# A new order inside the attention slots of an eight-core transformer layer

## Chip, cores and metric

The kernel runs on all eight cores of one Trainium2 chip. The time is that of the slowest core, in microseconds (us) on the device. The cores share nothing but the chip: each computes two of the sixteen sequences.

## The reference

The input is x of 16 sequences x 2048 tokens x 1024 features. One layer is computed:

```
n = layernorm(x)
Q, K, V = n@wq, n@wk, n@wv                        # 16 heads of 64
local   = softmax over a window of 256 earlier keys (blocks of 256) @ V
GQ, GK, GV = n@wgq, pool(n@wgk), pool(n@wgv)      # 8 heads of 64, 64 latents
rem     = softmax(GQ GK^T, causal over latents) @ GV @ r_out_w
out     = sigmoid(Q.gate_local) * local + sigmoid(Q.gate_remote) * rem
x       = x + out @ w_out
h = layernorm(x); for 3 blocks:                   # dequantized weights + lora
    h = linear(gelu(layernorm(linear(h)))) + h
x       = x + h
```

The weights of the feed-forward part are 4-bit integers with a scale for each group of 16, plus a product of two rank-32 matrices (lora).

## The kernel before

Each core works on 4096 tokens in eight tiles of 512 (`NJ = 8`, four to a sequence). There are three stages: the latent attention with its layernorm; the local attention (the stage of this change, about 355 to 1100 us of the span); and the feed-forward part. Every engine has a fixed list of instructions, written out by hand in the order of the source, and semaphores tie the lists together. An engine never passes over an instruction that waits.

The local attention goes through eight blocks, j = 0 to 7, one for each tile. A block begins with the values: eight units of eight matmuls (`values`, L451), with one unit for the gates (L483) in the middle. Then come eight slots, p = 0 to 7, one for each pair of heads; slot g = 8j + p. In a slot TensorE does, as far as the block has it:

- `bcast(g - 8)` (L427): two matmuls that spread the factors of the block before into S1, for VectorE's `mix`;
- `scores_a`, `scores_b`, `scores_c` of g + 1 (L361): key by query products with 64 rows of the array each, into S0, S1 and again S0;
- `project("k")` and `project("q")` (L349) of the next block, eight full-array matmuls each (blocks 0 to 6);
- `attend(g)` (L390 values, L399 denominators): matmuls with 64 columns of the array each, which need the masked exponentials of slot g;
- `lora` (L415), in slots 1 and 5, into S1: a weight slice for the feed-forward part;
- `wout(j - 2, p)` (L441): an eighth of the output projection of the block two before (blocks 2 to 7).

PSUM is shared out in units: S0 and S1 (1024 columns), O and D (512), and two units J0 and J1 of 512. k, q, wout, the values and the gates take J0 and J1 in turn, in the order of TensorE's list. Who takes a unit waits until its last user was read out (`drained`). k, q, values and the attention output are read out by ScalarE (`k_evac` L645, `evac` L592, L691, L711), the scores by its exponentials (`exp_a`, `exp_b`, `exp_p`, L656). wout is read out by VectorE (`resid`, L906: the addition of x, then statistics L908), which also masks the exponentials (`mask_a`, L863), multiplies by the broadcast factors (`mix`, L893, L894, L896), normalizes (`norm_a`, L918) and makes weight slices (`dequant_t` L925, `dequant_w` L934 or L944). ScalarE centres every other slice (`centre`, L674). After the eighth slot VectorE computes the factors of the block (`factor_a`, L876 to L885, with a reciprocal), and only then `resid(j - 2, 7)`.

SyncE's list (loads of x transposed and of the latent part, stores of x2 and its normalized form) and GpSimd's (loads of x and of weight slices) are the same in both kernels. They wait for `mixed`, `x2_done`, `xn2_done`, `dq_w` and `w_done`.

Of the kernel before, what the change touches and what calls it, by code (L numbers as in the profile page):

```python
# [20 lines left out]
NJ = NTOK // TT  # L21
# [13 lines left out]
A_K, A_Q, A_V, A_P = 0, 6144, 10240, 16384  # L35
# [38 lines left out]
def build_program():  # L74
# [38 lines left out]
    with contextlib.ExitStack() as es:  # L113
# [30 lines left out]
        a = lambda o, n: AR[:, o:o + n]  # L144
# [24 lines left out]
        junit = {}  # L169
# [84 lines left out]
        def pe(t):  # L254
# [89 lines left out]
            def project(kind, w, j, p):  # L344
                u = junit[kind, j, p] = nextj()
                k = u.take(kind, j, p)
                t.wait_ge(u.drained, k)
                for c in range(8):
                    mm = t.matmul(u.ap, w(c, p * 128, 128), xt(j % 2, c), start=(c == 0), stop=(c == 7))  # L349
                mm.then_inc(u.filled)  # L350
# [54 lines left out]
            def lora(n):  # L405
                i, c = DQ[n]
                lp = 32 * (i % 4)
                if n == 0:
                    t.wait_ge(ld_ca, 16 * 13)
                if n == 32:  # L410
                    t.wait_ge(ld_lalb2, 32)
                k = S1.take("lo", n)
                t.wait_ge(S1.drained, k)
                for hf in range(2):
                    mm = t.matmul(S1.ap[:, hf * 512:hf * 512 + 512], LALB[lp:lp + 32, c * 128:c * 128 + 128],  # L415
                                  LALB[lp:lp + 32, 1024 + hf * 512:1024 + hf * 512 + 512], start=True, stop=True)
                mm.then_inc(S1.filled)

            def bcast(g):

                j, p = divmod(g, 8)
                if p == 0:
                    t.wait_ge(f_done, j + 1)
                k = S1.take("bc", g)
                t.wait_ge(S1.drained, k)
                for side in range(2):
                    mm = t.matmul(S1.ap[:, side * 512:side * 512 + 512],  # L427
                                  SEL[:, (2 * p + side) * 128:(2 * p + side) * 128 + 128], a(A_F, 512),
                                  start=True, stop=True)
                mm.then_inc(S1.filled)  # L430
# [44 lines left out]
            for j in range(NJ):  # L475
                for n in range(8):
                    values(j, n)
                    if n == 3:
                        u = junit["z", j] = nextj()
                        k = u.take("z", j)  # L480
                        t.wait_ge(u.drained, k)
                        for c in range(8):
                            mm = t.matmul(u.ap, GZ[:, c * 128:c * 128 + 128], a(A_Q + c * 512, 512),  # L483
                                          start=(c == 0), stop=(c == 7))
                        mm.then_inc(u.filled)
                if j + 1 < NJ:
                    t.wait_ge(ld_xt[(j + 1) % 2], 16 * ((j + 1) // 2 + 1))
                for p in range(8):
                    g = 8 * j + p
                    if j >= 1:  # L490
                        bcast(g - 8)
                    if g + 1 < 8 * NJ:
                        scores_a(g + 1)
                    if j + 1 < NJ:
                        project("k", wk, j + 1, p)
                    if g + 1 < 8 * NJ:
                        scores_b(g + 1)
                    if p == 0:
                        for n in (6, 7):
                            u = junit["v", j, n]  # L500
                            t.wait_ge(u.drained, u.nth["v", j, n])
                    attend(g)
                    if g + 1 < 8 * NJ:
                        scores_c(g + 1)
                    if p in (1, 5):
                        lora(2 * j + p // 4)
                    if j + 1 < NJ:
                        project("q", wq, j + 1, p)
                    if j >= 2:
                        wout(j - 2, p)  # L510


            def y1(s, oc):
# [75 lines left out]
        def act(s):  # L589
# [95 lines left out]
            for j in range(NJ):  # L685
                for n in range(8):
                    u = junit["v", j, n]
                    tc, hf = divmod(n, 2)
                    vo = A_V + vslot(j, tc) * 1024 + hf * 512
                    s.wait_ge(u.filled, u.nth["v", j, n])  # L690
                    s.activation(a(vo, 512), u.ap, AF.Identity).then_inc(u.drained)  # L691
                    if n == 3:
                        u = junit["z", j]
                        s.wait_ge(u.filled, u.nth["z", j])
                        if j >= 1:
                            s.wait_ge(f_done, j)
                        s.activation(f32v(A_EZ, 512), u.ap, AF.Exp, scale=-1.0).then_inc(u.drained)
                for p in range(8):
                    g = 8 * j + p
                    if g + 1 < 8 * NJ:  # L700
                        exp_a(g + 1)
                    if j + 1 < NJ:
                        k_evac(j + 1, p)
                    if g + 1 < 8 * NJ:
                        exp_b(g + 1)
                    if p % 2 == 0 and 4 * (j - 2) + p // 2 - 1 >= 0:
                        rstd_a(4 * (j - 2) + p // 2 - 1)
                    if j >= 1:
                        s.wait_ge(mixed, g - 7)
                    s.wait_ge(UO.filled, UO.nth["av", g])  # L710
                    s.activation(a(A_O + p * 512, 512), UO.ap, AF.Identity).then_inc(UO.drained)  # L711
                    if g + 1 < 8 * NJ:
                        exp_p(g + 1, S0, "sc", 1024, 0)
                    if p == 2:
                        centre(2 * j)
                    if j + 1 < NJ:
                        evac(junit["q", j + 1, p], ("q", j + 1, p), a(A_Q + p * 512, 512))


            def y1_evac(sn, oc):  # L720
# [53 lines left out]
        def dve(v):  # L774
# [198 lines left out]
            for j in range(NJ):  # L973
                for p in range(8):
                    g = 8 * j + p
                    if j >= 1:
                        mix(g - 8)
                    if j >= 2 and p >= 1:
                        resid(j - 2, p - 1)
                    if p in (1, 5):  # L980
                        dequant_t(2 * j + p // 4)
                    if g + 1 < 8 * NJ:
                        mask_a(g + 1)
                    if p % 2 == 0 and 4 * (j - 2) + p // 2 - 1 >= 0:
                        norm_a(4 * (j - 2) + p // 2 - 1)
                    if p in (1, 5):
                        dequant_w(2 * j + p // 4)
                factor_a(j)
                if j >= 2:
                    resid(j - 2, 7)  # L990


            def square(sn, c):
# [384 lines left out]
```

## Time and profile before

| | |
|---|---|
| median of 3 runs | 1890.48 us (1888.58 to 1891.98) |
| the profiled execution | 1895.78 us, span of its slowest core 1894.3 us |
| spans of the eight cores | 1878.3 to 1894.3 us |
| VectorE busy | 1014.5 us, 54% |
| ScalarE busy | 837.0 us, 44% |
| load of 128 rows of x, issue to landing | 6.6 us |
| store of 128 rows of x2, issue to landing | 2.8 us |
| load of the scales of a weight slice, issue to landing | 8.4 us |

All rows are of core 0, the slowest. Matmuls are pipelined: 512 columns are issued every 0.22 us though one lasts 0.38. So starts are compared, not ends. Some matmul records are missing (a run of eight can show as x7).

A window's row gives: from and to, length, busy time of PE, PEld, DVE, ACT and POOL with their instructions, granted clock (1.00 is 2.4 GHz, and time at 1.2 GHz pulls it down), share of the DMA engines, GB/s. A timeline's row gives start, length, engine, line, shapes and count, and in brackets the idle time before it and who ended it.

### The profile page before, as it was taken

What the parts mean: (1) busy time and instruction counts of PE and PEld (TensorE: products, weight loads), DVE (VectorE), ACT (ScalarE), POOL (GpSimd) and SP (SyncE); (2) the same over time, 40 slices, a digit from 0 to 9 for tenths busy, and PEclk for the clock granted to TensorE, in tenths of its full rate; (3) what the DMA queues carried; (4) which work ended last, traced back from release to release, by engine and by line L of the source; (5) the groups of instructions that cost most, each with busy time, mean ns of one, the idle gap of its engine ahead of it and who ended that gap; (6) DMA issues with size and microseconds to landing.
All of it is one profiled execution on the core that took longest, in us unless ns stands there. A gap on an engine that the chain in (4) does not pass through costs nothing.

```text
span 1894.3 us, 26192 instructions; the slowest of 8 cores (1878.3 to 1894.3 us)
## 1 busy us (share of the span) xinstructions
PE 1606.5 (85%) x8828; PEld 722.4 (38%) x8994; DVE 1014.5 (54%) x1473; ACT 837.0 (44%) x1224; POOL 108.0 (6%) x191
## 2 busy tenths in 40 slices
PE   0347689999998989889875878999999899999998
PEld 0123233444443434444332333334434344444444
DVE  1346575044464656474656754555545656565555
ACT  0123345466454535445452145454444544444442
POOL 2000200000000000000000000000010000000000
PEclk9878899999999999999998989999999999999999
DMA  9986754611223233231358381211121121032223
GB/s 150 157 130 135 144 142 156 130 41 51 54 69 79 69 78 100 58 89 43 81 93 185 88 155 36 48 41 44 28 62 29 28 56 42 15 111 90 100 101 123
DMA packets 134353, 162.55 MB, mean 86 GB/s; under 512 B 80608, under 2 KB 92304, under 8 KB 131024
## 3 DMA queue, kind: packets, MB, share of 16 engines
q1 hardware_dynamic: 100128, 97.02, 19.1%
q0 software_dynamic: 34096, 63.85, 18.9%
q8 instruction: 76, 1.25, 0.3%
q14 instruction: 53, 0.43, 0.1%
HBM read 123.91 MB, written 52.43 MB: 93 GB/s over the span
## 4 chain that ended last, share of the span: by engine, by line
PE 58%; DVE 15%; DVEq 6%; issue 6%; DMA 6%; SPq 5%; ACT 5%; ACTq 0%; POOL 0%; POOLq 0%
PE ps L524 14%; PE ps L349 10%; PE ps L451 6%; PE ps L549 6%; PE ps L554 4%; SPq L1192 4%; DMA XT<-AR 4%; PE ps L441 3%; DVE AR L1004 3%; PE ps L361 3%; DVEq L931 2%; PE ps L532 2%; PE ps L390 2%; PE ps L399 2%; DVE WA L809 2%
## 5 line engine op out<-in xcount | busy, mean ns | idle before, releaser
L524 PE MATMUL ps<-WA,WB 128*128 128x512 bf16 x1003 | 234.2, 389 | 27.2 <-ACT AR L724 21.8
L349 PE MATMUL ps<-XT,WA 128*128 128x512 bf16 x967 | 231.2, 381 | 7.8 <-issue 7.1
L656 ACT ACTIVATE AR<-ps 128x1024 bf16<-128x1024 f32 (+2 forms) x192 | 186.1, 970 | 99.9 <-PE ps L361 97.7
L740 ACT ACTIVATE AR<-AR,LNB,LNG 128x512 bf16<-128x512 bf16 x192 | 145.6, 806 | 154.0 <-DVE AR L1004 153.8
L724 ACT ACTIVATE AR<-ps,CB 128x512 bf16<-128x512 f32 x192 | 128.8, 683 | 181.3 <-PE ps L524 181.3
L290 PE MATMUL ps<-XT,WB 128*128 128x512 bf16 x254 | 69.0, 438 | 129.2 <-DMA XT<-AR 129.0
L524 PEld LDWEIGHTS ps<-WA,WB 128*128 128x128 bf16 x1024 | 101.0, 100 | 155.7 <-issue 45.4
L592 ACT ACTIVATE AR<-ps 128x512 bf16<-128x512 f32 x96 | 57.3, 597 | 207.3 <-PE ps L290 158.1
L863 DVE TENSOR_TENSOR AR<-AR,MLOC 128x3072 bf16<-128x3072 bf16 x48 | 84.4, 1759 | 109.9 <-ACT AR L656 109.9
L451 PE MATMUL ps<-WA,XT 128*128 128x512 bf16 x509 | 122.8, 400 | 23.6 <-DVE AR L906 23.5
L349 PEld LDWEIGHTS ps<-XT,WA 128*128 128x128 bf16 x1024 | 91.2, 98 | 121.5 <-issue 27.9
L441 PE MATMUL ps<-WA,AR 128*128 128x512 bf16 x503 | 123.2, 390 | 16.5 <-DVE AR L906 15.6
L1012 DVE SCALAR_TENSOR_TENSOR WA<-ps,BIAS,WA 128x512 bf16<-128x512 f32 x128 | 95.7, 748 | 76.3 <-PE ps L549 76.2
L554 PE MATMUL ps<-XT,AR 128*128 128x512 bf16 x498 | 121.6, 385 | 8.2 <-DVE AR L1028 4.0
L999 DVE TENSOR_TENSOR AR<-AR 128x512 bf16<-128x512 bf16 x192 | 73.5, 422 | 100.3 <-ACT AR L724 99.4
L925 DVE SCALAR_TENSOR_TENSOR AR<-AR 128x1024 f32<-128x1024 int8 x48 | 58.3, 1219 | 127.8 <-DMA AR<-scT 127.8
L1004 DVE TENSOR_TENSOR AR<-AR 128x512 bf16<-128x512 bf16 x192 | 123.5, 686 | 6.1 <-issue 6.1
L524 PE MATMUL ps<-WA,AR 128*128 128x512 bf16 x503 | 114.3, 383 | 13.1 <-ACT AR L724 12.6
L549 PE MATMUL ps<-AR,XT 128*128 128x512 bf16 x500 | 116.4, 379 | 4.1 <-DVE WA L1012 3.5
L549 PE MATMUL ps<-AR 128*128 128x512 bf16 x499 | 116.2, 379 | 4.1 <-DVE WA L1012 3.5
L893 DVE TENSOR_TENSOR AR<-ps,AR 128x512 bf16<-128x512 f32 x64 | 44.2, 690 | 115.9 <-PE ps L427 115.1
L290 PEld LDWEIGHTS ps<-XT,WB 128*128 128x128 bf16 x256 | 27.7, 110 | 170.1 <-issue 148.8
(134 smaller groups left out, 1988.6 us busy)
## 6 DMA issues: line engine op xcount, KB each, us to landing
AR<-scT POOLq DMA_DIRECT2D x48, 512.0 KB, 8.4
AR<-x_in POOLq DMA_DIRECT2D x64, 256.0 KB, 6.6
y<-AR SPq DMA_DIRECT2D x32, 512.0 KB, 2.9
xnT<-XT SPq DMA_DIRECT2D x8, 1024.0 KB, 3.9
remT<-AR SPq DMA_DIRECT2D x8, 1024.0 KB, 6.2
XT<-xnT SPq DMA_DIRECT2D x8, 1024.0 KB, 5.3
AR<-remT SPq DMA_DIRECT2D x64, 128.0 KB, 3.5
x<-AR SPq DMA_DIRECT2D x32, 256.0 KB, 2.8
```

What stands on the lines that cost most here:

```text
L290: mm = t.matmul(u.ap, WB[:, c * 512 + oc * 128:c * 512 + oc * 128 + 128], xt(par, c), start=(c == 0), stop=(c == 7))
L349: mm = t.matmul(u.ap, w(c, p * 128, 128), xt(j % 2, c), start=(c == 0), stop=(c == 7))
L441: mm = t.matmul(u.ap, a(A_MIX + (j % 2) * 4096 + c * 512 + sub * 128, 128), wo(c, hf * 512, 512), start=(c == 0), stop=(c == 7))
L451: mm = t.matmul(u.ap, xt(j % 2, c, tc * 128, 128), wv(c, hf * 512, 512), start=(c == 0), stop=(c == 7))
L524: mm = t.matmul(u.ap, wmat(2 * k3, c, oc * 128, 128), rt(tt, c), start=(c == 0), stop=(c == 7))
L549: mm = t.matmul(u.ap, wmat(2 * k3 + 1, c, oc * 128, 128), a(yb + c * 512, 512), start=(c == 0), stop=(c == 7))
L554: t.matmul(u.ap, a(yb + c * 512 + sub * 128, 128), wmat(5, c, hf * 512, 512), start=(c == 0), stop=False)
L656: s.activation(dst[:, :, col + lo:col + hi], src[:, :, lo:hi], AF.Exp, scale=ISQ).then_inc(u.drained)
L724: s.activation(a(B_Y1 + (sn % 2) * 4096 + oc * 512, 512), u.ap, AF.Identity, bias=CB[:, 8 * i + oc:8 * i + oc + 1]).then_inc(u.drained)
L740: s.activation(yb, yb, AF.Gelu, bias=LNB[:, 8 * i + c:8 * i + c + 1], scale=LNG[:, 8 * i + c:8 * i + c + 1]).then_inc(g_done)
L1004: v.tensor_tensor(yb, yb, f32v(B_RS, 512), op=ALU.mult).then_inc(yn_done)
L1012: v.scalar_tensor_tensor(rt(tt, oc), u.ap, BIAS[:, 8 * i1 + oc:8 * i1 + oc + 1], rt(tt, oc), op0=ALU.add, op1=ALU.add).then_inc(u.drained)
```

## The change

The order inside a slot is rewritten on three engines. TensorE does the output unit, k, lora and q right after the broadcast, then scores a and b, the attention, scores c. ScalarE does the statistics of the second layernorm, k, q and the centring first, then the exponentials a and b, the attention output, c. VectorE adds the residual of the slot's own output unit, not of the slot before, so that the eighth one comes in slot 7, ahead of `factor_a`; `dequant_w`, `norm_a` and, in slot 7, `factor_a` go before the mask, and `dequant_t` moves from slots 1 and 5 to the ends of slots 0 and 4.

```diff
@@ TensorE
                     if j >= 1:
                         bcast(g - 8)
+                    if j >= 2:
+                        wout(j - 2, p)
+                    if j + 1 < NJ:
+                        project("k", wk, j + 1, p)
+                    if p in (1, 5):
+                        lora(2 * j + p // 4)
+                    if j + 1 < NJ:
+                        project("q", wq, j + 1, p)
                     if g + 1 < 8 * NJ:
                         scores_a(g + 1)
-                    if j + 1 < NJ:
-                        project("k", wk, j + 1, p)
-                    if g + 1 < 8 * NJ:
                         scores_b(g + 1)
...
                     attend(g)
                     if g + 1 < 8 * NJ:
                         scores_c(g + 1)
-                    if p in (1, 5):
-                        lora(2 * j + p // 4)
-                    if j + 1 < NJ:
-                        project("q", wq, j + 1, p)
-                    if j >= 2:
-                        wout(j - 2, p)
@@ ScalarE
                     g = 8 * j + p
+                    if p % 2 == 0 and 4 * (j - 2) + p // 2 - 1 >= 0:
+                        rstd_a(4 * (j - 2) + p // 2 - 1)
+                    if j + 1 < NJ:
+                        k_evac(j + 1, p)
+                        evac(junit["q", j + 1, p], ("q", j + 1, p), a(A_Q + p * 512, 512))
+                    if p == 2:
+                        centre(2 * j)
                     if g + 1 < 8 * NJ:
                         exp_a(g + 1)
-                    if j + 1 < NJ:
-                        k_evac(j + 1, p)
-                    if g + 1 < 8 * NJ:
                         exp_b(g + 1)
-                    if p % 2 == 0 and 4 * (j - 2) + p // 2 - 1 >= 0:
-                        rstd_a(4 * (j - 2) + p // 2 - 1)
                     if j >= 1:
                         s.wait_ge(mixed, g - 7)
                     s.wait_ge(UO.filled, UO.nth["av", g])
                     s.activation(a(A_O + p * 512, 512), UO.ap, AF.Identity).then_inc(UO.drained)
                     if g + 1 < 8 * NJ:
                         exp_p(g + 1, S0, "sc", 1024, 0)
-                    if p == 2:
-                        centre(2 * j)
-                    if j + 1 < NJ:
-                        evac(junit["q", j + 1, p], ("q", j + 1, p), a(A_Q + p * 512, 512))
@@ VectorE
                     if j >= 1:
                         mix(g - 8)
-                    if j >= 2 and p >= 1:
-                        resid(j - 2, p - 1)
+                    if j >= 2:
+                        resid(j - 2, p)
                     if p in (1, 5):
-                        dequant_t(2 * j + p // 4)
+                        dequant_w(2 * j + p // 4)
+                    if p % 2 == 0 and 4 * (j - 2) + p // 2 - 1 >= 0:
+                        norm_a(4 * (j - 2) + p // 2 - 1)
+                    if p == 7:
+                        factor_a(j)
                     if g + 1 < 8 * NJ:
                         mask_a(g + 1)
-                    if p % 2 == 0 and 4 * (j - 2) + p // 2 - 1 >= 0:
-                        norm_a(4 * (j - 2) + p // 2 - 1)
-                    if p in (1, 5):
-                        dequant_w(2 * j + p // 4)
-                factor_a(j)
-                if j >= 2:
-                    resid(j - 2, 7)
+                    if p in (0, 4):
+                        dequant_t(2 * j + p // 4)
```

## Rows read from the trace of the kernel before

**Rows 1.** The page, busy time of TensorE, its share of the span.
```profile
PE 1606.5 (85%) x8828; PEld 722.4 (38%) x8994; DVE 1014.5 (54%) x1473; ACT 837.0 (44%) x1224; POOL 108.0 (6%) x191
```

**Rows 2.** Windows, core 0: values after block 0; slots 1, 2; values; slots 4; values; slots 7.
```profile
421.12:436.66 15.54, 15.49 (x73) 7.02 (x73) 7.46 (x6) 5.37 (x9) 0.00 (x0) 1.00 0.01 1
436.66:495.88 59.22, 53.71 (x429) 25.03 (x436) 30.89 (x38) 38.09 (x49) 2.36 (x4) 0.97 0.24 63
...
511.43:579.42 67.99, 65.94 (x493) 30.97 (x500) 44.12 (x59) 39.94 (x56) 3.95 (x7) 1.00 0.33 86
579.42:602.12 22.70, 17.93 (x73) 7.54 (x73) 7.04 (x8) 4.78 (x8) 0.00 (x0) 0.85 0.05 12
...
691.63:755.35 63.72, 62.19 (x434) 28.49 (x441) 42.04 (x67) 35.59 (x58) 4.48 (x8) 1.00 0.40 102
...
936.11:957.97 21.86, 17.09 (x73) 7.26 (x73) 7.04 (x8) 4.78 (x8) 0.00 (x0) 0.92 0.05 14
957.97:1015.70 57.73, 39.15 (x347) 19.95 (x352) 40.23 (x55) 28.39 (x38) 3.14 (x6) 0.94 0.81 139
```
**Rows 3.** Timeline of TensorE, first slot of block 5: start, length, line, count.
```profile
777.72 0.39 PE L361 MATMUL ps<-AR 64*128 64x384 bf16 x4
778.05 1.90 PE L349 MATMUL ps<-XT,WA 128*128 128x512 bf16 x7
779.88 0.39 PE L361 MATMUL ps<-AR 64*128 64x256 bf16 x4
780.20 0.85 PE L390 MATMUL ps<-AR 128*64 128x256 bf16 x12
780.88 0.82 PE L399 MATMUL ps<-AR,OHD 128*64 128x256 bf16 x12
781.64 0.39 PE L361 MATMUL ps<-AR 64*128 64x384 bf16 x4
781.96 1.90 PE L349 MATMUL ps<-XT,WA 128*128 128x512 bf16 x8
783.70 1.89 PE L441 MATMUL ps<-WA,AR 128*128 128x512 bf16 x8
```

**Rows 4.** Timeline of ScalarE, the same slot, and the centring of slot 2.
```profile
780.04 0.60 ACT L645 ACTIVATE AR<-ps 128x512 bf16<-128x512 f32 x1 [0.81 <-PE ps L349]
780.54 1.02 ACT L656 ACTIVATE AR<-ps 128x1024 bf16<-128x1024 f32 x1
781.44 0.29 ACT L667 ACTIVATE RST<-MV,COLS 128x1 f32<-128x1 f32 x1
...
781.95 0.60 ACT L711 ACTIVATE AR<-ps 128x512 bf16<-128x512 f32 x1
782.44 1.02 ACT L656 ACTIVATE AR<-ps 128x1024 bf16<-128x1024 f32 x1
...
801.24 1.15 ACT L674 ACTIVATE WB<-AR,RSUM 128x1024 bf16<-128x1024 f32 x1
```

**Rows 5.** Timeline of VectorE, mask of the first slot to the scale product of the second.
```profile
783.56 1.76 DVE L863 TENSOR_TENSOR AR<-AR,MLOC 128x3072 bf16<-128x3072 bf16 x1 [3.85 <-ACT AR L656]
785.24 0.54 DVE L918 TENSOR_SCALAR AR<-AR,MV,RST 128x1024 bf16<-128x1024 bf16 x1
786.13 0.69 DVE L893 TENSOR_TENSOR AR<-ps,AR 128x512 bf16<-128x512 f32 x1 [0.35 <-PE ps L427]
786.73 0.68 DVE L894 TENSOR_TENSOR AR<-ps,AR 128x512 bf16<-128x512 f32 x1
...
787.86 0.68 DVE L906 TENSOR_TENSOR AR<-ps,AR 128x512 bf16<-128x512 f32 x1
...
789.24 1.21 DVE L925 SCALAR_TENSOR_TENSOR AR<-AR 128x1024 f32<-128x1024 int8 x1
```

**Rows 6.** Timeline of VectorE, end of block 5, behind the factor chain: the eighth residual.
```profile
850.97 0.68 DVE L906 TENSOR_TENSOR AR<-ps,AR 128x512 bf16<-128x512 f32 x1
```

**Rows 7.** Timeline of TensorE, the second unit of values after block 5.
```profile
851.80 7.85 PE L451 MATMUL ps<-WA,XT 128*128 128x512 bf16 x24 [4.72 <-DVE AR L906]
```

## The prediction

> **What bounds the kernel now.** I read the page first: PE is busy for 85% of the span [rows 1], so I took PE's order of work for the clock of the attention stage and asked where it stands still. The windows of the stage, cut at the starts of the value matmuls, answer that [rows 2]. A stage of eight slots of blocks 2 to 6 takes 68.0 us (63.7 in block 4, where a sequence starts and less is masked), PE is busy for 97% of them, at clock 1.00. The values stage after blocks 0 and 1 takes 15.5 us; the five that follow blocks 2 to 6 take 22.70 (first) to 21.86 us (last), 111.0 together, although the same 72 matmuls run: in each, PE stops after its first unit for 4.4 to 4.85 us [rows 7] and runs on at a lower clock (0.85 to 0.92 over the stage). The row names VectorE's L906, the residual addition of the eighth output unit. VectorE started it only behind the factor chain [rows 6]. So two things can be won: these gaps, and small seams inside a slot. I then wrote down one slot by the timelines of the three engines [rows 3 to 5], because what decides is whether the new order leaves ScalarE and VectorE time to answer.
>
> **The change on PE.** Eight full-array matmuls in a row take 1.74 us (781.96 to 783.70), but 1.83 when half-array scores follow, and scores worth 0.22 us of columns take 0.33 before a full-array run [rows 3]. A seam between full-array and half-array work costs 0.10 us. Before, a slot has six: broadcast to scores a, a to k, k to b, b to values, denominators to c, c to q. After, four: q to a, b to values, denominators to c, c to the next broadcast. 0.2 us a slot, over the 56 slots of blocks 0 to 6 11 us, less one seam more for each of 14 lora pairs (1.4): about 10 us. Row and rule: the Trainium skill, "TensorEngine Tiling (Array Packing)", section Key Properties, says that a change of tiling mode drains TensorE. The trace agrees, with 0.10 us; by that rule alone the change only wins, and this is the first rival below.
>
> New slot of PE, from the first q matmul: q 1.74, seam 0.10, scores a and b 0.22 each, seam 0.10, values 0.68, denominators with seam 0.76, last scores with seam 0.32 [rows 3]: 4.14, then two broadcasts 0.43, output unit 1.74, k 1.74. Without a wait that is 8.05 us.
>
> **What the other two need.** ScalarE's order is now k, q, scores a, scores b, attention output, scores c. Counted from the start of q: its evacuation starts 2.00 later (k: 778.05 to 780.04), the exponential of a 0.50 after that, b 0.90 after a, the output evacuation 0.90 after b, c 0.49 after that: 4.79 [rows 3, 4]. It lasts 1.02, and the mask starts 1.12 after its start (782.44 to 783.56): 5.91. The next VectorE instruction starts 1.68 later: 7.59 [rows 5]. That is the mix of the next slot, for the mask is queued ahead of it on VectorE. From the mix's first product to the residual's addition are 1.73 us (786.13 to 787.86): 9.32. PE goes on 0.83 after the start of such an addition (850.97 to 851.80) [rows 6, 7]: 10.15.
>
> What waits for that addition? The two J units alternate. Output unit, k and q are taken in turn, so q of a slot has the unit that this slot's output matmuls filled, and waits for their residual. Before, the residual of an output unit had until the q matmuls of the next slot; now it has only the 1.74 us of k, and lies behind mask and mix. So from q to q a slot of blocks 2 to 6 takes 10.15 us, 2.1 above PE's own 8.05. Behind the waiting q on PE stand the scores and the attention of the slot, so the exponentials start late too, and the next mask with them: the loop closes. Part of that shows ahead of the broadcast: its unit S1 is freed by the exponential of b, which ends 3.40 + 1.02 after q, plus 0.15 to PE (851.80 less the end of the 0.68 us addition), 4.57 against 4.14.
>
> Extras in a block: the scale product of a weight slice (1.21 us, [rows 5]) stands between mask and mix after slots 0 and 4: 2.4. Centring (L674, 1.15 us, the next start some 1.05 later, [rows 4]) stands ahead of the exponentials in slot 2: 1.05. The lora pair and its VectorE step lie within the wait. Block: 3.91 to the first q, 7 x 10.15 = 71.05, 3.5, and 4.14 after the last q: 82.6 against 68.0: +14.6, four times 58.4. Block 4 scaled by 63.7/68.0: +13.7. Together +72.1.
>
> **Queues of the DMAs.** The residual comes a slot earlier, so loads of x have less time: a tile's load can go once the norm of two tiles before is stored, some two slots (20 us) ahead, and store and load take 2.8 + 6.6 us in the page. A weight slice is loaded after the centring of slot 2 and wanted at the end of slot 4, again 20 us against 8.4. SyncE's and GpSimd's lists are the same; I cost this at nothing. Were slots to shrink under 5 us it would show.
>
> Block 1 has no output unit. There the wait on S1 paces it: 4.57 + 0.43 + 1.74 = 6.74 from q to q, five times. In slots 1 and 5 lora waits for the mix to free S1: 7.59 + 1.21 + 0.60 + 0.68 + 0.15 = 10.23, and 0.53 to q: 10.76, twice. With 2.17 ahead, 4.14 behind and centring 1.05: 62.6 against 59.22 [rows 2]: +3.4. Bounds: -3 if the waits for lora vanish, +6 if the clock falls behind them.
>
> Block 0: seams -1.6 and centring ahead of the exponentials +1.1: -0.5. Block 7 has no projections: PE already waits there for the mix to free S1, 57.73 us at clock 0.94 [rows 2]; the cycle scores b, exponential, output, c, mask, mix is the same in both orders (about 6.45 us), and the weight step moves from the broadcast's wait to that of scores b. I take 0, bounds -4 and +4. The tail after it is tied to stores and loads of x that keep their order: 0, bounds -3 and +3.
>
> **What is won.** The residual of the eighth unit now goes before the factor chain, so its J unit is free before the values start. The five values stages return to 15.54 us: 111.0 - 77.7 = -33.3. What is late next there: the masks of the next block now follow the chain, but the attention that needs them comes 17 us later; nothing.
>
> **Clock.** Blocks 2 to 6 will stand for a fifth of the time. The rows show 1.00 where PE is busy for 97%, 0.97 at 91% (block 1) and 0.94 at 68% (block 7) [rows 2]. I take 0.96 for them: 3.3 us of PE's work more in a block, of which some fifth (q, of the slot's work) lies on the cycle: +3 in all. Bounds 0 and +20.
>
> Sum: 72.1 + 3.4 - 0.5 - 33.3 + 3 = +45, to 1940.5 on the profiled execution (1895.8 us, 1.5 beyond its span). That is 5.3 above the median of the runs, so I forecast 1935 as median. Its own range, 1912 to 1965.
>
> **Rivals.** (1) Seams and gaps only: the addition is never awaited, PE runs through. Then 33 + 10 are won: 1847. For it: VectorE has slack, since it is busy for some 6 of 8 us. Against: slack isn't order; the mask ends at 7.6 after q whatever the load. Decides: whether mask ends before the next output unit does (6.7 after q). Chance 3%.
> (2) Only the wait on S1 is left, because the residual is there in time: ScalarE or VectorE runs its short list faster than the sum of starts above. Slots of 4.57 + 3.91 = 8.48: block 3.91 + 59.4 + lora 1.3 + 1.05 + 4.14 = 69.8, +1.8 in five blocks, 9 in all; with +3.4 - 0.5 - 33.3: 1869, faster than before. The point from which it decides: the cycle must be under 8.9 us, where a block takes 11.55 + 7 x 8.9 = 73.8, 5.8 more than before, five times 28, and the gaps pay for it. Chance 8%.
> (3) The clock falls with the waits. A stall of 2.1 us a slot comes just ahead of q, and if all 35 q runs on the cycle go at 1.2 GHz instead of 2.4, each costs 1.74 more: +61, 1993. Against it: block 7 waits 1.2 to 3.1 us in every slot and keeps 0.94. The Trainium skill, "TensorE: Matmul & The Clock Gate", section "A second HAM failure mode: psum-queue depth-cycling", describes this: short idle spells between matmul groups make the clock swing. Chance 7%.
> (4) PE's seams and orders cancel, no change: a cycle of about 8.9. Chance 3%.
>
> **Numbers.** Forecast 79%. 1908 to 1965 leaves out rivals 1 to 3 and little of the forecast. A difference under 0.2% (3.8 us) can't be told from none. Faster: rivals 1 and 2, 11%. Same: 3%. Slower: the rest, 86%.
>
> **What would show it.** Right: in slots of blocks 2 to 6 PE waits 1.6 to 1.8 us before L349 (q) for DVE L906, and about 0.4 before L427 for ACT L656; first q to first q of the next slot 10.1 us; slots' stages near 82.6 us; no wait before L451, values stages 15.5 us; VectorE's L893 starts right behind L863. Wrong: L906 starts as soon as the output unit is full, or the waits stand at the scores.

## The result, and the profile after

The changed kernel takes 1961.17 us (median of four runs, 1957.38 to 1969.89), the kernel before 1890.48 on the same chip (median of three): a ratio of 1.038 (95% interval 1.033 to 1.043), slower. The forecast was 1935, its range 1908 to 1965. All comparisons leave runs out in which the cores of one die were disturbed.

The profiled execution took 1957.38 us. Its slowest core is core 1, with a span of 1955.9 us; all rows of after are of that core. In its numbering L903 is the addition of the residual (L906 before), L890 and L891 the first two products of the mix, L860 the mask, L655 an exponential, L922 the scale product and L941 the weight step. First the page's busy line, which answers to [rows 1].

```profile
PE 1621.1 (83%) x8994; PEld 726.9 (37%) x8994; DVE 1010.3 (52%) x1473; ACT 828.4 (42%) x1224; POOL 108.0 (6%) x191
```

TensorE's share fell by only two points and VectorE has no more work than before. Nothing here says where 70 us went. The windows do; they are cut at the same places as [rows 2]: slots of blocks 0 and 1, slots 2, values, slots 4, 5 and 7.

```profile
372.93:421.67 48.74, 45.17 (x362) 21.24 (x360) 15.18 (x21) 31.89 (x56) 2.36 (x4) 1.00 0.18 55
...
437.22:504.93 67.71, 58.93 (x438) 27.18 (x436) 30.39 (x38) 35.98 (x49) 2.36 (x4) 0.90 0.18 55
...
520.48:603.95 83.47, 68.51 (x502) 32.03 (x500) 42.93 (x61) 36.62 (x54) 3.95 (x7) 0.98 0.27 73
603.95:619.50 15.55, 15.55 (x77) 7.07 (x74) 7.56 (x6) 6.48 (x11) 0.00 (x0) 1.00 0.00 1
...
718.40:797.84 79.44, 66.84 (x442) 29.20 (x440) 41.23 (x69) 32.26 (x56) 4.48 (x8) 0.96 0.32 87
...
813.39:898.96 85.57, 69.78 (x502) 32.37 (x500) 43.38 (x62) 36.89 (x56) 4.48 (x8) 0.96 0.30 81
...
1013.53:1078.77 65.24, 44.85 (x361) 21.63 (x359) 41.87 (x59) 28.11 (x38) 2.79 (x5) 0.82 0.81 127
```

Every values stage now takes 15.54 or 15.55 us. Every stage of slots is longer. The same cuts on core 1 of both kernels give this account; the slots' stages of before agree on all eight cores within 0.4 us, its long values stages within 1. The changed kernel's do not: over the cores slots 1 take 64.0 to 67.7 us, slots 5 83.8 to 85.8, slots 7 62.5 to 66.0.

| stage | before | after | difference | predicted |
|---|---|---|---|---|
| slots 0 | 45.8 | 48.7 | +2.9 | -0.5 |
| slots 1 | 59.3 | 67.7 | +8.4 | +3.4 |
| slots 2 to 6 | 335.5 | 415.3 | +79.8 | +72.1, clock +3 |
| slots 7 | 57.8 | 65.2 | +7.4 | 0 |
| values behind blocks 2 to 6 | 111.6 | 77.7 | -33.9 | -33.3 |
| sum | | | +64.6 | +45 |

The spans of core 1 differ by 72.5 us. Of the other 7.9, the feed-forward part holds 5.3 and the tail after slot 7 the rest. One part of the row of slots 7 is no loss: the stage ends with the last attention, and the eighth output unit (1.74 us) lay behind that point before and lies ahead of it now. Like with like, block 7 lost 5.7 us and the tail 1.7 more than the cut shows. On core 0 the feed-forward part goes the other way (835.3 us before, 827.2 after), so I count it as spread between executions and not as the change's.

An ordinary slot of block 2 (no lora pair) answers to [rows 3]. TensorE's timeline, from its broadcast to the k matmuls of the next slot:

```profile
561.54 0.59 PE L427 MATMUL ps<-AR,SEL 128*128 128x512 bf16 x2 [0.37 <-ACT AR L655]
561.97 1.89 PE L441 MATMUL ps<-WA,AR 128*128 128x512 bf16 x8
563.70 1.89 PE L349 MATMUL ps<-XT,WA 128*128 128x512 bf16 x8
567.13 1.89 PE L349 MATMUL ps<-XT,WA 128*128 128x512 bf16 x8 [1.54 <-DVE AR L903]
568.95 0.61 PE L361 MATMUL ps<-AR 64*128 64x384 bf16 x8
...
573.84 1.89 PE L349 MATMUL ps<-XT,WA 128*128 128x512 bf16 x8
```

ScalarE's in the same slot:

```profile
569.11 0.60 ACT L591 ACTIVATE AR<-ps 128x512 bf16<-128x512 f32 x1 [2.83 <-PE ps L349]
569.61 1.94 ACT L655 ACTIVATE AR<-ps 128x1024 bf16<-128x1024 f32 x2
...
571.89 1.06 ACT L655 ACTIVATE AR<-ps 128x1024 bf16<-128x1024 f32 x1
```

And VectorE's:

```profile
562.91 1.76 DVE L860 TENSOR_TENSOR AR<-AR,MLOC 128x3072 bf16<-128x3072 bf16 x1 [4.96 <-ACT AR L655]
564.58 0.68 DVE L890 TENSOR_TENSOR AR<-ps,AR 128x512 bf16<-128x512 f32 x1
...
566.30 0.68 DVE L903 TENSOR_TENSOR AR<-ps,AR 128x512 bf16<-128x512 f32 x1
...
573.05 1.76 DVE L860 TENSOR_TENSOR AR<-AR,MLOC 128x3072 bf16<-128x3072 bf16 x1 [4.83 <-ACT AR L655]
```

Follow the loop: q starts at 567.13, its evacuation at 569.11, the exponentials at 569.61, the last of them at 571.89, the mask at 573.05. In the slot before, the mask started at 562.91, the mix 1.67 later, the addition 1.72 after that, and q 0.83 after the addition. The loop is 5.92 + 1.67 + 1.72 + 0.83 = 10.14 us, and from k to k TensorE takes 10.14. VectorE stands idle for almost 5 us ahead of each mask: the engine on which everything waits is itself waiting half of the time.

The groups of waits on TensorE, 355 to 1080 us. In PSUM (ps), L349 is q, L415 lora, L427 the broadcast, L361 the scores; the numbers are total us, count, longest:

```profile
PE ps L349 <- DVE AR L903: 42.9, 35, 1.9
PE ps L415 <- DVE AR L891: 30.9, 14, 6.0
PE ps L427 <- ACT AR L655: 10.0, 26, 0.5
PE ps L361 <- ACT AR L655: 7.2, 8, 1.1
```

In the slots with a lora pair, 1 and 5, the wait is divided in two, and the q matmuls behind it often run at the lower clock. Slot 1 of block 5:

```profile
827.43 0.59 PE L415 MATMUL ps<-LALB 32*128 32x512 bf16 x2 [1.55 <-DVE AR L891]
828.55 3.40 PE L349 MATMUL ps<-XT,WA 128*128 128x512 bf16 x8 [0.53 <-DVE AR L903]
```

The eight q matmuls took 3.40 us, not 1.89. On core 1 q is slow (2.7 to 3.6 us) in 7 of the 10 lora slots of blocks 2 to 6, and never behind the 25 undivided waits of 1.3 to 1.9 us. Added up it costs 9.1 us, all of it in the loop (4.9 to 9.1 over the cores).

### The profile page after: what moved, and what is told of

Read it like the earlier page. It is cut to its first block, busy times and chain, and to the rows that moved or that the text cites. A ratio compares the mean times of both kernels' runs of the same rounds, so it can differ in the third digit from the quotient of the medians.

```text
span 1955.9 us, 26358 instructions; the slowest of 8 cores (1932.5 to 1955.9 us)
## 1 busy us (share of the span) xinstructions
PE 1621.1 (83%) x8994; PEld 726.9 (37%) x8994; DVE 1010.3 (52%) x1473; ACT 828.4 (42%) x1224; POOL 108.0 (6%) x191
## 4 chain that ended last, share of the span: by engine, by line
PE 49%; DVE 14%; DVEq 9%; ACT 8%; issue 7%; DMA 7%; SPq 5%; ACTq 1%; POOL 0%; POOLq 0%
PE ps L523 13%; PE ps L349 9%; PE ps L451 6%; PE ps L548 5%; DVEq L892 4%; PE ps L553 4%; SPq L1188 4%; ACT AR L655 4%; DMA XT<-AR 4%; DVE AR L1000 3%; PE ps L531 2%; PE ps L390 2%; DVEq L904 2%; PE ps L361 2%; PE ps L274 1%
## 5 line engine op out<-in xcount | busy, mean ns | idle before, releaser
L349 PE MATMUL ps<-XT,WA 128*128 128x512 bf16 x1024 | 249.5, 393 | 42.9 <-DVE AR L903 42.9
L655 ACT ACTIVATE AR<-ps 128x1024 bf16<-128x1024 f32 (+2 forms) x192 | 181.6, 979 | 34.0 <-PE ps L361 33.6
L860 DVE TENSOR_TENSOR AR<-AR,MLOC 128x3072 bf16<-128x3072 bf16 x48 | 84.3, 1757 | 187.1 <-ACT AR L655 187.1
L349 PEld LDWEIGHTS ps<-XT,WA 128*128 128x128 bf16 x1024 | 99.1, 100 | 180.2 <-issue 75.6
L922 DVE SCALAR_TENSOR_TENSOR AR<-AR 128x1024 f32<-128x1024 int8 x48 | 58.4, 1221 | 134.0 <-DMA AR<-scT 133.8
L451 PE MATMUL ps<-WA,XT 128*128 128x512 bf16 x512 | 113.2, 379 | 0.0
L361 PE MATMUL ps<-AR 64*128 64x384 bf16 (+1 forms) x704 | 67.8, 287 | 21.5 <-ACT AR L655 7.2
```

The lines of the kernel that those rows point to most:

```text
L361: mm = t.matmul(u.ap[:, hh * 512 + col:hh * 512 + col + nq * 128], AR[rows, kcl:kcl + 128], AR[rows, A_Q + p * 512 + q0 * 128:A_Q + p * 51 ...
L451: mm = t.matmul(u.ap, xt(j % 2, c, tc * 128, 128), wv(c, hf * 512, 512), start=(c == 0), stop=(c == 7))
L655: s.activation(dst[:, :, col + lo:col + hi], src[:, :, lo:hi], AF.Exp, scale=ISQ).then_inc(u.drained)
```

## Experiments

Each ratio is to the kernel before on the same chip, with its 95% interval. The first four ran on one chip, the next three on one, the last two on one.

### 1. The residual ahead of the factor chain alone

The kernel before, with the one move on VectorE that frees the eighth output unit.

```diff
-                factor_a(j)
                 if j >= 2:
                     resid(j - 2, 7)
+                factor_a(j)
```

> The kernel before with one edit: the residual of the eighth output unit goes ahead of the factor chain. By my account the five gaps of the values stages (4.4 to 4.85 us each, and the slow clock behind them) go: each values stage 15.5 us instead of 21.7 to 22.9, in sum 33 us, so about 1857 us, and the slots stay at 68.0 us a block. The rival, that the gap is made by the attention's end or by the evacuations and the residual only closes it, gives 1885 to 1891 us with another wait ahead of the second values unit.

Measured: 1861.8 and 1865.4 us, ratio 0.982 (0.975 to 0.989). Windows of core 3, slots 2 and the values behind them:

```profile
509.62:577.61 67.99, 67.20 (x501) 30.96 (x500) 43.70 (x58) 39.98 (x56) 3.95 (x7) 1.00 0.32 86
577.61:593.15 15.54, 15.54 (x73) 7.06 (x72) 7.63 (x8) 4.79 (x8) 0.00 (x0) 1.00 0.07 19
```

Beside [rows 2], the slots are the same to 0.01 us and the values lose their gap, at clock 1.00. This half of the change is worth some 33 us, as computed (about 1857 us was forecast). So the rest of it costs about 100.

### 2. The mask behind the mix and the residual

The loop's longest link taken out: VectorE adds the residual before it masks.

```diff
                     if j >= 2:
                         resid(j - 2, p)
+                    if g >= 1:
+                        mask_a(g)
...
-                    if g + 1 < 8 * NJ:
-                        mask_a(g + 1)
```

> The changed kernel with one edit on VectorE: the mask of a slot's exponentials goes behind that slot's mix and residual instead of ahead of them (the same instructions, one place later in the list). If the loop mask, mix, residual, q is what costs, q no longer waits for the residual; what is left is the broadcast's wait for the exponential of scores b, so q to q falls from 10.15 to about 8.5 us, a block's slots from 83.6 to about 70, block 1 from 67.6 to about 56, block 7 from 65 to about 50: 1865 to 1875 us. If instead the loss comes from the burst of scores on PE and ScalarE or from the clock, and the wait for the residual is only where it shows, the waits turn up elsewhere and the time stays within 10 us of 1961.

Measured: 1885 us (1879.0 to 1888.9), ratio 0.994 (0.991 to 0.996). Windows of core 3, slots 1, 2 and 7, and a group of waits:

```profile
437.79:494.22 56.43, 52.28 (x438) 25.70 (x436) 32.08 (x39) 35.63 (x48) 2.36 (x4) 1.00 0.24 66
...
509.77:580.99 71.22, 66.22 (x501) 32.24 (x500) 45.11 (x62) 37.41 (x55) 3.94 (x7) 1.00 0.33 86
...
937.93:1014.84 76.91, 48.41 (x361) 24.30 (x359) 45.66 (x62) 28.90 (x40) 4.47 (x8) 0.82 0.65 122
...
PE ps L390 <- DVE AR L860: 20.1, 8, 4.1
```

One move on one engine takes 12 to 15 us from each of blocks 2 to 6 (83.5 to 71.2 in block 2): the mask's place is the cause of the loop. The 76 us between this kernel and the changed one (84 by the two ratios, for they ran on different chips) are the largest effect of any single edit here. The forecast, 1865 to 1875 us, missed because of block 7, where I had expected 50 us and 77 came (73.7 to 77.0 over the cores). There is no projection there to cover the mask: the attention itself now waits for it (six of the eight waits, 19.5 us, are in block 7), scores b wait 4.5 us for the weight step in each of slots 1 and 5, and the clock fell to 0.82.

### 3. The output unit behind q

The other way to open the loop: TensorE fills the J unit only after q has taken its own.

```diff
-                    if j >= 2:
-                        wout(j - 2, p)
...
                     if j + 1 < NJ:
                         project("q", wq, j + 1, p)
+                    if j >= 2:
+                        wout(j - 2, p)
```

> The changed kernel with one edit on TensorE: the output unit is computed behind q instead of ahead of k, so it is the q of the next slot that takes its J unit, 8 us later. VectorE's order stays as it is, mask ahead of mix. By the theory that the J unit carries the loop, the wait of q for the residual is gone and the slots of blocks 2 to 6 are paced by the broadcast's wait for scores b, 8.3 to 8.5 us a slot: some 80 us less in five blocks, 1880 us; blocks 1 and 7 keep their waits for S1 (67.6 and about 65 us). By the rival that mask ahead of mix costs the slot anyway through S1 (scores b then wait for the mix), slots stay near 10 us and the time near 1955 us.

Measured: 1984.6 us, ratio 1.046 (1.041 to 1.052): the forecast of 1880 missed by over 100. TensorE on core 0, two output units in a row, then the lora pair and scores b of slot 1:

```profile
555.52 1.89 PE L441 MATMUL ps<-WA,AR 128*128 128x512 bf16 x8
...
563.80 1.89 PE L441 MATMUL ps<-WA,AR 128*128 128x512 bf16 x8
...
573.80 0.59 PE L415 MATMUL ps<-LALB 32*128 32x512 bf16 x2 [3.29 <-DVE AR L891]
...
583.22 0.40 PE L361 MATMUL ps<-AR 64*128 64x256 bf16 x4 [3.26 <-DVE AR L941]
```

And VectorE in that slot:

```profile
579.74 0.69 DVE L903 TENSOR_TENSOR AR<-ps,AR 128x512 bf16<-128x512 f32 x1 [5.57 <-PE ps L441]
...
581.85 1.22 DVE L941 SCALAR_TENSOR_TENSOR AR<-AR,ps 128x1024 bf16<-128x1024 f32 x1 [0.31 <-issue]
```

The ordinary slot did what I had worked out (8.28 us, no wait before q anywhere), which confirms the J unit as the link. But I had not followed slots 1 and 5. There the weight step that frees S1 is queued on VectorE behind the residual, the residual waits 5.57 us for the output unit, which is now late, and scores b wait for S1. The slot takes 17.1 us. On core 1, the slowest, the clock goes to between 0.87 and 0.90 in four of the five blocks (0.94 in block 4), a block takes up to 90.4 us, and block 7 takes 75.0 us in place of 65.2.

### 4. An order without the loop

TensorE in blocks 2 to 6: output unit, k, broadcast, q, scores a and b, attention, scores c, and lora last. VectorE: residual's addition, mask, mix, statistics, norm, scale product and weight step.

```diff
@@ TensorE
-                    if j >= 1:
+                    if j == 1 or j == NJ - 1:
                         bcast(g - 8)
...
                         project("k", wk, j + 1, p)
-                    if p in (1, 5):
-                        lora(2 * j + p // 4)
+                    if 2 <= j < NJ - 1:
+                        bcast(g - 8)
...
                         scores_c(g + 1)
+                    if p in (1, 5):
+                        lora(2 * j + p // 4)
@@ VectorE
-                    if j >= 1:
+                    if j == 1 or j == NJ - 1:
                         mix(g - 8)
                     if j >= 2:
-                        resid(j - 2, p)
...
+                        resid_x(j - 2, p)
+                    if g >= 1:
+                        mask_a(g)
+                    if 2 <= j < NJ - 1:
+                        mix(g - 8)
```

> A version that should beat both. In blocks 2 to 6 TensorE does output unit, k, broadcast, q, scores a and b, attention, scores c, lora; VectorE adds the residual first, then masks, then mixes, with the statistics last; blocks 1 and 7 keep the broadcast first with mask behind mix; centring goes to the end of ScalarE's slot, both steps of a weight slice to the end of VectorE's. By the sum of starts no wait is left in a slot of blocks 2 to 6 except about 0.5 us ahead of lora: 8.1 us a slot, 66 to 67 us a block, values stages 15.5, together 1840 to 1850 us. If PE's bursts or ScalarE set a floor that I don't see, slots stay at 8.5 us or more and the time at 1865 or above.

Measured: 1848.9, 1854.4 and 1862.1 us (1840 to 1850 was forecast), ratio 0.978 (0.971 to 0.984). On core 5, windows of slots 2 and 7, and a group of waits (L862 is the mask here):

```profile
511.51:577.55 66.04, 65.30 (x502) 32.12 (x500) 44.78 (x62) 36.50 (x54) 3.95 (x7) 1.00 0.32 87
...
916.08:985.77 69.69, 42.39 (x362) 22.98 (x361) 45.28 (x62) 28.64 (x40) 4.46 (x8) 0.88 0.89 136
...
PE ps L390 <- DVE AR L862: 24.2, 8, 8.3
```

Slots 2 take 66.0 us, 2.0 under [rows 2], and an ordinary slot 8.02 us, where the prediction had 8.05 for TensorE without waits. So the gain of fewer seams is real: some 2 us a block, 8.7 in five blocks (326.8 us on core 5 against 335.5). Block 7 gives that back, for its attention waits for the masks, as in experiment 2. Part of the loss has another cause: on the three cores (0, 3, 4) where no load of x came late, block 7 takes 61.3 to 63.4 us, on the others 65.8 to 70.9. On core 5 the residual, which is queued ahead of the mask, waits 6.0 us for a load of x, and the longest wait above, 8.3 us, is the one behind it.

### 5 and 6. Load on VectorE off and on the loop

One more pass over 128 x 1024 elements in every slot of blocks 2 to 6, written to room that nothing reads: ahead of the mask in 5 (shown), where VectorE is idle, and right behind it in 6.

```diff
+                    if 2 <= j < NJ - 1:
+                        v.drain()
+                        v.tensor_tensor(a(A_D2, 1024), MLOC[:, 0:1024], MLOC[:, 0:1024], op=ALU.mult)
                     if g + 1 < 8 * NJ:
                         mask_a(g + 1)
```

> The changed kernel with one more pass of VectorE (128x1024 bf16 product into unused room, about 0.7 us with the drain before it) in each slot of blocks 2 to 6, put ahead of the mask, that is, behind the residual and its statistics, where VectorE waits for the exponentials. If the cycle mask, mix, residual, q sets the pace, this pass isn't on it: the slots stay at 10.14 us and the time within 5 us of the changed kernel's (1957 to 1965 us). If VectorE's amount of work is what counts, it costs the same as the next kernel's pass, 25 us.

Measured: 1963 us, ratio 1.035 (1.033 to 1.037), against 1.038 for the change without the pass. Core 1, the waits before q:

```profile
PE ps L349 <- DVE AR L903: 42.3, 35, 1.9
```

Forty passes cost nothing: blocks 2 to 6 take 413.1 us on this core, 415.3 without the passes, and over the eight cores the means are 414.1 and 413.9. (Block 7 took 72.5 us on this core, for the scales of a weight slice came 8.5 us late; on the other cores it took 62.7 to 67.7.)

> The same pass, put behind the mask, that is, between mask and mix. By the theory each of the 35 steps from q to the next q in blocks 2 to 6 grows by the whole pass and its drain, 0.7 to 0.9 us: 25 to 32 us more, 1985 to 1995 us, the slots at 10.9 to 11.0 us. If there is slack on the cycle, less than 10 us more.

Measured: 2007 us, ratio 1.058 (1.056 to 1.060): 44 us more than experiment 5 on the same chip, where 25 to 32 was forecast. The groups of waits before q and before lora, core 1:

```profile
PE ps L349 <- DVE AR L903: 61.7, 35, 2.6
PE ps L415 <- DVE AR L891: 37.1, 14, 4.4
```

And the q matmuls of one slot, core 3:

```profile
576.91 2.74 PE L349 MATMUL ps<-XT,WA 128*128 128x512 bf16 x8 [2.34 <-DVE AR L903]
```

An ordinary slot takes 10.93 us in place of 10.14: the pass and the drain before it, 0.79 us, are paid in full. So the place on VectorE sets the time, not the load. On core 1 blocks 2 to 6 take 458.3 us, 43.0 more than in the changed kernel. Forty slots at 0.79 are 31.6 of that. The rest is the clock: behind waits of 2.34 us the q matmuls shown took 2.74 us in place of 1.89, and such slow groups add up to 21.0 us on core 1, 11.9 more than in the changed kernel. The five stages have a granted clock of 0.93 to 0.96 on core 3.

### 7. Blocks 0, 1 and 7 one by one

Experiment 4, with lora ahead of q in blocks 0 and 1, and in block 7 the order of the kernel before on TensorE and VectorE.

```diff
+                    if j < 2 and p in (1, 5):
+                        lora(2 * j + p // 4)
...
+                    if j == NJ - 1:
+                        wout(j - 2, p)
```

> The new order of e4 in blocks 2 to 6 (66.0 us of slots), block 1 with lora ahead of q as in e2 (56.4 us there, 59 to 61 in e4), block 7 in the order of the kernel before with its eighth residual ahead of the factors (57.8 us there, 61 to 71 in e4, where the attention waited for a mask behind the mix). By the sum 3 us less in block 1 and 4 to 10 in block 7: 1844 to 1850 us. If block 7's time is set by the loads of the transposed operand that share its stretch and not by the order, it stays above 61 us and the time at e4's 1858.

Measured: 1857.8 us, ratio 0.980 (0.978 to 0.982), where 1844 to 1850 was forecast. Block 7 takes 64.5 us, not 58. ScalarE's timeline, core 0, the statistics, which stand ahead of the exponentials:

```profile
952.19 0.29 ACT L672 ACTIVATE RST<-MV,COLS 128x1 f32<-128x1 f32 x1 [5.42 <-DVEq L920]
```

I had put two engines back and left the third. ScalarE still has the layernorm's statistics at the head of the slot, ahead of the exponentials, and they wait 5.42 us for a residual that VectorE, in the old order, adds a slot later.

### 8. Block 7 in the old order on all three engines

Experiment 4, with block 7 as before and the eighth residual ahead of the factor chain.

```diff
-                    if p % 2 == 0 and 4 * (j - 2) + p // 2 - 1 >= 0:
+                    if p % 2 == 0 and 4 * (j - 2) + p // 2 - 1 >= 0 and j < NJ - 1:
                         rstd_a(4 * (j - 2) + p // 2 - 1)
...
                         exp_b(g + 1)
+                    if p % 2 == 0 and j == NJ - 1:
+                        rstd_a(4 * (j - 2) + p // 2 - 1)
```

> e4 with block 7 in the order of the kernel before on all three engines (output unit last, mask of the next slot behind the mix, ScalarE's statistics behind the exponentials), its eighth residual ahead of the factors. e7 had this on TensorE and VectorE only, and its first exponential of a slot stood behind statistics that now come later: 64.5 us. If the order is what sets block 7, it returns to 57 to 61 us, against 61 to 70 in e4, and the time of the slowest core falls from 1858 to 1846 to 1852 us. If the clock or the loads of the transposed operand set it, the block stays above 62 us and the time within 3 us of e4's.

Measured: ratio 0.977 (0.971 to 0.982), 1851.4 to 1878.2 us. Window of slots 7, core 4:

```profile
920.13:980.06 59.93, 42.92 (x354) 20.52 (x353) 40.20 (x56) 28.39 (x38) 2.79 (x5) 0.89 0.80 135
```

The stage is back at 59.2 to 60.4 us over the cores, as forecast. This order has the eighth output unit behind the cut again, so it compares with 57.8 us before and with 63.5 (65.2 less 1.74) in the changed kernel: most of block 7's loss is that of the order. The time is not as forecast: 1846 to 1852 us was forecast, and the median of the six runs is 1858.8. The kernel as a whole can't be told from experiment 4. The two are the fastest here, but their intervals overlap that of experiment 1, too.

### 9. The scale product off the lora path

The changed kernel, with the scale product of a weight slice next to its weight step, so that it no longer stands ahead of the mix.

```diff
                     if p in (1, 5):
+                        dequant_t(2 * j + p // 4)
                         dequant_w(2 * j + p // 4)
...
-                    if p in (0, 4):
-                        dequant_t(2 * j + p // 4)
```

> The changed kernel with the scale product of a weight slice (1.21 us) taken from behind the mask of slots 0 and 4 and put ahead of the weight step in slots 1 and 5. By the theory the waits of lora for the mix fall by 1.2 us each (3.3 to 2.1 us in blocks 1 and 7), but scores b then wait some 1.2 us longer for the weight step in the same slots, so that blocks 2 to 6 gain at most 1.5 us each; the 2.67 us for which VectorE waited for a weight slice in block 7 go too. Sum: 5 to 15 us less than 1961, 1946 to 1956. If lora's waits come from somewhere else than VectorE's order, they stay at 3.3 us and the time at 1961.

Measured: 1952.4 us (1946.3 to 1958.3), ratio 1.026 (1.021 to 1.032). TensorE in block 1 of the changed kernel, a lora pair and the q matmuls behind it:

```profile
449.54 1.01 PE L415 MATMUL ps<-LALB 32*128 32x512 bf16 x2 [3.28 <-DVE AR L891]
450.48 3.59 PE L349 MATMUL ps<-XT,WA 128*128 128x512 bf16 x8
```

The same in this experiment, with the window of slots 1:

```profile
449.92 0.59 PE L415 MATMUL ps<-LALB 32*128 32x512 bf16 x2 [2.15 <-DVE AR L891]
450.44 1.90 PE L349 MATMUL ps<-XT,WA 128*128 128x512 bf16 x8
...
438.74:499.03 60.29, 53.30 (x437) 25.72 (x436) 30.40 (x38) 35.65 (x49) 2.36 (x4) 1.00 0.22 61
```

On this core two waits are 1.13 us shorter each, 2.3 together, but block 1 is 7.4 us shorter. The other 5 are the clock: behind both waits of 3.28 us eight matmuls took 3.59 us, at the lower of its two levels, and behind both of 2.15 they took 1.90. The stage's clock went from 0.90 to 1.00. But the shorter wait did not settle it. On six of the eight cores of the same execution one of the two groups still ran slowly, as on core 0:

```profile
447.54 0.59 PE L415 MATMUL ps<-LALB 32*128 32x512 bf16 x2 [2.15 <-DVE AR L891]
448.06 3.55 PE L349 MATMUL ps<-XT,WA 128*128 128x512 bf16 x8
```

Block 1 takes 60.3 to 61.9 us over the cores, and 64.0 to 67.7 in the changed kernel. In its blocks 2 to 6 the waits ahead of lora fell to 0.4 us, and no q group behind a lora pair was slow.

## Why the prediction was right, and by how much it missed

The forecast was 1935 us and 1961 came: 26 us short, of which 20 lie in the attention stage as core 1 shows it.

**The mechanism** was right, step for step. Evacuation 2.00 us after q was predicted and 1.98 measured; mask 5.91 and 5.92; mix 1.68 later and 1.67; residual 1.73 and 1.72; q 0.83 and 0.83; the loop 10.15 and 10.14. The broadcast waits 0.37 us for the exponential of b, about 0.4 predicted; q waits 1.54, just under the 1.6 to 1.8 predicted. Experiments 2 (mask moved: the wait goes), 3 (output unit moved: the ordinary slot is 8.28 us) and 6 (a pass on the loop: paid in full) each break or stretch one link, and 5 excludes VectorE's load.

**The gaps** ahead of the values: -33.3 predicted, -33.9 measured, and alone in experiment 1. **The seams**: 8.05 us for a slot without waits predicted, 8.02 in experiment 4. The gaps' gain shows in the changed kernel itself; the seams' gain is measured only in experiment 4, for in the changed kernel TensorE waits anyway. The Trainium skill, "TensorEngine Tiling (Array Packing)", section Key Properties, has the drain at a change of tiling mode and no more. The trace agrees, with 0.10 us a seam. By that rule alone the change wins, and that rival (1847) fell, as rival 2 (1869) did: a loop through three engines outweighed it.

**Terms that were mis-sized**, 20 us in all (64.6 over the attention stage, not 45):

- Block 7, 0 predicted, +7.4 measured, of which 1.7 is the output unit that changed sides of the cut. I compared the cycle of the two orders and took them for equal, since the same instructions were in it. But lora had moved ahead of the scores and the weight step ahead of the mask, and a weight slice's load is wanted earlier. TensorE in slot 5:

```profile
1060.14 1.01 PE L415 MATMUL ps<-LALB 32*128 32x512 bf16 x2 [5.97 <-DVE AR L891]
...
1063.91 0.61 PE L361 MATMUL ps<-AR 64*128 64x256 bf16 x4 [2.21 <-DVE AR L941]
```

  and VectorE ahead of it, the scale product:

```profile
1057.57 1.23 DVE L922 SCALAR_TENSOR_TENSOR AR<-AR 128x1024 f32<-128x1024 int8 x1 [2.67 <-DMA AR<-scT]
```

  The step that said the DMA queues cost nothing reckoned with slots of 10 us and a load of 8.4 us. Block 7's slots are some 8 us, this load took 13.5 us from issue to landing (7.9 to 9.4 in blocks 5 and 6), and the DMA engines are busy for 81% of the stage. So the scales came 2.67 us late. The cores divide the loss roughly: on the four where nothing came late (2, 3, 5, 7) block 7 takes 62.5 to 63.9 us, on the other four 64.1 to 66.0. Experiment 8 shows that the old order takes the stage back to 59.2 to 60.4. The clock also fell, from 0.94 to 0.82 in this stage; its price was not measured by itself.
- Block 1, +3.4 predicted, +8.4 measured. Its waits came as computed; the clock behind them was put down as a bound (+6) and happened. Experiment 9 puts the clock's part on core 1 at some 5 us, which is the whole miss.
- Blocks 2 to 6, +72.1 and +3 for the clock predicted, +79.8 measured. The term that was too small is the clock's: the slow q groups behind lora pairs cost 9.1 us on core 1. Without them +70.7 is left, for the 72.1 of the loop. I had taken a clock of 0.96 and a fifth of TensorE's work on the loop. The clock stayed higher (0.96 to 0.98), but the slow matmuls came right behind the waits, so all of them were on the loop. They also explain why block 5 (85.6) is 2 us longer than blocks 2, 3 and 6, and block 4 longer than I had scaled it (79.4 against 77.4): in those two both lora slots have a slow q, in the others one.
- Block 0, -0.5 predicted, +2.9 measured. Scores b wait 1.07 us for the weight step in each of slots 1 and 5, a wait I had put nowhere in this block. The other 1.3 us stay open.

**Rival 3**, the clock: 0.96 taken, 0.96 to 0.98 measured in blocks 2 to 6. In the ordinary slots, waits of 1.5 us never lowered it, so the price of 61 us did not come. But the mechanism exists: it took 9.1 us in the lora slots of blocks 2 to 6, some 5 in block 1, and 21.0 in blocks 2 to 6 of experiment 6, where the waits are 0.8 us longer. The Trainium skill, "TensorE: Matmul & The Clock Gate", section "A second HAM failure mode: psum-queue depth-cycling", describes a clock that swings because of short idle spells between groups of matmuls. This trace shows that in part: in block 1, in the lora slots and in experiment 6 it holds, in the ordinary slots of blocks 2 to 6 it does not.

## What to carry to other kernels

Where engines run fixed lists, write down for each shared buffer who holds it, who frees it, and what stands ahead of the freeing instruction in its own list, and add that up round the loop; 5.4 us of VectorE work in a slot of 10.4 us says nothing. A change that takes the largest blocks of one engine together can win its seams (8.7 us here) and lose some ten times that in answers that come too late; moving the one instruction that frees the buffer kept the better part of the gain (experiment 1). Work each kind of slot through by itself, those with extra instructions and those with fewer above all: the misses whose cause was found, of the prediction and of experiments 2, 3 and 7, were in such slots.

## What the runs showed of the hardware

TensorE's clock fell behind short waits, but the length of a wait alone did not say when. These are the groups of eight q matmuls behind a wait, over all eight cores of the profiled executions. A slow group took 2.3 to 3.6 us in place of 1.89:

| wait ahead of q | where | slow groups |
|---|---|---|
| 1.2 to 1.9 us, undivided | changed kernel, blocks 2 to 6 | 0 of 200 |
| 1.3 to 1.6 us, the lora pair, 0.53 us more | changed kernel, blocks 2 to 6 | 48 of 80 |
| 2.0 to 2.7 us, undivided | experiment 6, blocks 2 to 6 | 89 of 200 |
| 2.15 us, then the lora pair | experiment 9, block 1 | 6 of 16 |
| 3.3 us, then the lora pair | changed kernel, block 1 | 15 of 16 |

The same wait in the same place could end either way on two cores of one execution. So an added pass of 0.7 us cost 44 us in one place and nothing in another: on core 1, 31.6 of its 43 were the loop and some 12 the clock. A wait should be priced at its length, with slower matmuls behind it as a second term with its own bound; that term was some 11 of the 20 us by which this prediction missed.
